# State product ahead of the attention product in a fused attention and expert layer: TensorE's order in a step turned round, the state sum in another bank, and two VectorE operations moved up

## What is computed

```python
q, k = elu(rope(q) * SCALE) + 1, elu(rope(k) * SCALE) + 1          # of layernorm(x) @ w_qkv
kv[t] = kv[t-1] + k[t] (x) v[t];   ks[t] = ks[t-1] + k[t]          # the running state, per head
out[t] = (q[t] @ kv[t]) / max(q[t] . ks[t], 1e-6)
x = x + out @ w_out
h = silu(n @ Wg[e]) * (n @ Wu[e])                                  # n = layernorm(x), e = 0..7
x = x + sum over e of weight[t, e] * (h @ Wd[e])                   # weights from a small router
```

## Time and profile before

| | us |
|---|---|
| median of 3 runs | 805.64 |
| the profiled execution | 806.51 |
| its span, first to last instruction | 804.7 |
| TensorE matmuls (PE) busy | 761.0 (95%) |
| TensorE weight loads (PEld) busy | 655.0 (81%) |
| VectorE (DVE) busy | 603.9 (75%) |
| GpSimd (POOL) busy | 482.7 (60%) |
| ScalarE (ACT) busy | 465.1 (58%) |

### The profile page before, as it was taken

The page is one execution under the profiler, slowest core; times in us unless marked ns, Lnnn a source line. Parts: engine busy times, 40 slices in busy tenths (PEclk is TensorE's granted clock), DMA queues, the critical chain, the costliest instruction groups (busy, mean ns, idle before and its releaser), DMA issues.

```text
span 804.7 us, 18060 instructions
## 1 busy us (share of the span) xinstructions
PE 761.0 (95%) x6660; PEld 655.0 (81%) x6660; DVE 603.9 (75%) x1597; ACT 465.1 (58%) x886; POOL 482.7 (60%) x537
## 2 busy tenths in 40 slices
PE   4475899999999999999999999999999999999998
PEld 3364688888888888888888888888888888888887
DVE  6788797878877797778877697877877788756244
ACT  3664666666666555566665566666656665634222
POOL 3685678765666666556667565565675656653322
PEclk9666799999999999999999999999999999999999
DMA  4644134122210222122111221120211121100000
GB/s 140 128 100 109 43 82 92 41 43 68 40 19 23 44 66 41 41 43 38 44 27 40 43 67 40 41 42 9 60 42 40 40 54 28 28 1 27 1 1 27
DMA packets 97320, 38.27 MB, mean 48 GB/s; under 512 B 74193, under 2 KB 96977, under 8 KB 97233
## 3 DMA queue, kind: packets, MB, share of 16 engines
q1 hardware_dynamic: 90704, 30.83, 17.8%
q10 hardware_dynamic: 6528, 6.29, 2.7%
HBM read 16.13 MB, written 4.19 MB: 25 GB/s over the span
## 4 chain that ended last, share of the span: by engine, by line
PE 88%; DVE 5%; POOL 2%; ACT 2%; issue 1%; DMA 1%; SPq 0%; DVEq 0%; ACTq 0%; POOLq 0%
PE gate L422 22%; PE y L455 22%; PE up L422 21%; PE front L297 5%; PE back L342 3%; PE front L298 3%; PE back L378 2%; PE back L353 2%; PE up L390 1%; PE front L320 1%; PE front L403 1%; PE back L335 1%; PE back L365 1%; POOL a_lo L1167 1%; PE back L320 1%
## 5 line engine op out<-in xcount | busy, mean ns | idle before, releaser
L1196 POOL TENSOR_TENSOR h_lo<-work,h_hi 128x512 fp32r<-128x512 f32 x126 | 163.3, 1296 | 59.7 <-ACT h_hi L657 59.7
L1167 POOL TENSOR_TENSOR a_lo<-am,a_hi 128x512 f16<-128x512 f32 x120 | 144.2, 1203 | 55.3 <-ACT a_hi L584 52.6
L455 PE MATMUL y<-wd_hi,h_hi 128*128 128x256 f32 x504 | 145.8, 289 | 0.0
L455 PE MATMUL y<-wd_lo,h_hi 128*128 128x256 f32 x504 | 141.9, 282 | 0.0
L455 PE MATMUL y<-wd_hi,h_lo 128*128 128x256 f32 x504 | 141.3, 280 | 0.0
L1040 DVE TENSOR_TENSOR work<-work,up 128x512 f32<-128x512 f32 x128 | 87.1, 680 | 70.6 <-PE up L422 70.2
L1056 DVE SCALAR_TENSOR_TENSOR xa<-y,wo,xa 128x256 f32<-128x256 f32 x252 | 111.9, 470 | 2.0 <-PE y L455 2.0
L657 ACT ACTIVATE h_hi<-work 128x512 fp32r<-128x512 f32 x126 | 79.3, 629 | 58.6 <-DVE work L1040 37.0
L455 PEld LDWEIGHTS y<-wd_lo,h_hi 128*128 128x128 f32 x504 | 94.9, 188 | 3.0
L455 PEld LDWEIGHTS y<-wd_hi,h_hi 128*128 128x128 f32 x504 | 95.0, 188 | 2.9
L584 ACT ACTIVATE a_hi<-am 128x512 f16<-128x512 f32 x120 | 74.9, 625 | 35.1 <-DVE am L819 35.0
(11 more groups left out here) (217 smaller groups left out, 1740.2 us busy)
## 6 DMA issues: line engine op xcount, KB each, us to landing
xr<-xT SPq DMA_DIRECT2D x32, 128.0 KB, 2.4
xa<-x SPq DMA_DIRECT2D x32, 128.0 KB, 2.6
out<-xa SPq DMA_DIRECT2D x32, 128.0 KB, 1.7
xa<-Wg ACTq DMA_DIRECT2D x8, 256.0 KB, 3.0
work<-Wd ACTq DMA_DIRECT2D x8, 256.0 KB, 2.7
work<-Wu ACTq DMA_DIRECT2D x8, 256.0 KB, 2.9
work<-w_qkv SPq DMA_DIRECT2D x2, 384.0 KB, 3.8
qT<-q_st SPq DMA_TRANSPOSE x32, 3.2
```

What stands on the lines that cost most here:

```text
L455: m = pe.matmul(y_bank(n, t), h_at(hi, n)[:, t * P:(t + 1) * P], wd_p[wi][:, u // KI, u % KI, :], start=(n % KI == 0 and (t % 2 == 0 or n ...
L1167: pool.tensor_tensor(a_p[1][:, heads(r), :], am_place(g, r).rearrange("p (h n) -> p h n", h=4), a_p[0][:, heads(r), :], ALU.subtract).then ...
L1196: pool.tensor_tensor(h_at(1, n), hb[:, n % 2, :], h_at(0, n).bitcast(F32), ALU.subtract).then_inc(s_hlo, 1)
```

## The change

On TensorE `state(c)` goes from behind `o_T(c)` to the front of `av(c)`. Its sum goes to bank U instead of R2 for tiles from 4 on; so it waits for `h_up(n)`, the last reader of that bank, and `up(n + 1)`, the next writer, waits for `st_add(c)`. Within `av` of those tiles the part from the state comes last instead of first; both halves of the sum are announced by the last two matmuls. On VectorE `h_up(n)` moves from behind `cos(a)` to ahead of `var_eps(a + 1)`, and `st_add(c)` from behind `h_up(n + 1)` to between `cos(a)` and `rope(a)`. The head keeps its order. No instruction is added or taken out but waits.

```diff
+        def state_bank(g):
+            return R2 if g < NT else U
@@ av(g)
-                w.wait_ge(s_s3, g)
                 w.wait_ge(s_amask, 4 * g + 4)
                 w.wait_ge(s_v3, g + 1)
-                for p in range(NP):
-                    for odd in range(2):
-                        rows = slice(64 * odd, 64 * odd + 64)
-                        pe.matmul(BK[odd][:, p * WV:(p + 1) * WV], qT[rows, g % 2, p, :],
-                                  st_x[rows, p, :, :].rearrange("p a b -> p (a b)"),
-                                  start=(p == 0), stop=False, skip_group_check=True)
+                def from_state(first, last):
+                    w.wait_ge(s_s3, g)
+                    for p in range(NP):
+                        for odd in range(2):
+                            rows = slice(64 * odd, 64 * odd + 64)
+                            m = pe.matmul(BK[odd][:, p * WV:(p + 1) * WV], qT[rows, g % 2, p, :],
+                                          st_x[rows, p, :, :].rearrange("p a b -> p (a b)"),
+                                          start=(first and p == 0), stop=(last and p == NP - 1), skip_group_check=True)
+                            if last and p == NP - 1:
+                                m.then_inc(s_av, 1)
+                if g < NT:
+                    from_state(True, False)
                 w.wait_ge(s_alo, 4 * g + 4)
                 for odd in range(2):
                     for p in range(NP):
-                        for a in a_p:
+                        for i, a in enumerate(a_p):
                             m = pe.matmul(BK[odd][:, p * WV:(p + 1) * WV], a[:, 2 * p + odd, :],
                                           vx[:, g % 2, 2 * p + odd, :, :].rearrange("p a b -> p (a b)"),
-                                          start=False, stop=(p == NP - 1), skip_group_check=True)
-                    m.then_inc(s_av, 1)
+                                          start=(g >= NT and p == 0 and i == 0), stop=(g < NT and p == NP - 1),
+                                          skip_group_check=True)
+                    if g < NT:
+                        m.then_inc(s_av, 1)
+                if g >= NT:
+                    from_state(False, True)
@@ state(g)
-                w.wait_ge(s_o, 2 * g + 1)
+                w.wait_ge(s_v3, g + 1)
+                if g < NT:
+                    w.wait_ge(s_o, 2 * g + 1)
+                else:
+                    w.wait_ge(s_h, NT * (g - NT) + 1)
...
-                        m = pe.matmul(R2[:, p * 2 * W1:(p + 1) * 2 * W1],
+                        m = pe.matmul(state_bank(g)[:, p * 2 * W1:(p + 1) * 2 * W1],
@@ up(n)
                 w.wait_ge(s_h, n)
+                w.wait_ge(s_ss, 2 * min((n + NT - 1) // NT + NT, NTL))
@@ TensorE's step
-                logit_rows(router); gate(n); logit(router); up(n); qkv(a); gate(n + 1); av(c); down(n - 2)
-                up(n + 1); down(n - 1); o_T(c); state(c); gate(n + 2); proj(c); up(n + 2); gate(n + 3); down(n)
+                logit_rows(router); gate(n); logit(router); up(n); qkv(a); gate(n + 1); state(c); av(c); down(n - 2)
+                up(n + 1); down(n - 1); o_T(c); gate(n + 2); proj(c); up(n + 2); gate(n + 3); down(n)
@@ VectorE's step
-                mean_var(a + 1); tcos_scale(a); x_lo(a + 1); acc(n - 4, 1); acc(n - 4, 2); acc(n - 4, 3)
-                var_eps(a + 1); route_zone(router); route_nearest(router); cos(a); h_up(n); rope(a); o_sum(c, 0)
+                mean_var(a + 1); tcos_scale(a); x_lo(a + 1); acc(n - 4, 1); acc(n - 4, 2); acc(n - 4, 3); h_up(n)
+                var_eps(a + 1); route_zone(router); route_nearest(router); cos(a); st_add(c); rope(a); o_sum(c, 0)
                 o_sum(c, 1); den_max(c); phi(a); route_weight(router); den_rec(c); slab_lo(slab(s, 1))
                 route_first(router); norm(c); route_second(router); q_lo(a); k_lo(a); o_lo(c); h_up(n + 1)
-                st_add(c); route_tie(router); x1_add(c); acc(n - 2, 0); bn2(c); route_ix2(router); acc(n - 2, 1)
+                route_tie(router); x1_add(c); acc(n - 2, 0); bn2(c); route_ix2(router); acc(n - 2, 1)
```

More of the change, by code:

```diff
@@ L151, in build @@
         oT = R3[:, 0:D].rearrange("p (k n) -> p k n", k=KD)
-        stp = R2[:, 0:NP * 2 * W1].rearrange("p (q h d) -> p q h d", q=NP, h=2)
         io = bcast(iota[:, :], 1, NT)
@@ L847, in st_add @@
                 w.wait_ge(s_state, g + 1)
+                stp = state_bank(g)[:, 0:NP * 2 * W1].rearrange("p (q h d) -> p q h d", q=NP, h=2)
                 for hh in range(2):
```

## The result

The changed kernel takes 804.22 us (median of 14 runs, 803.15 to 805.23) against 805.5 us (14 runs, 804.5 to 807.11); ratio 0.9981, 95% interval 0.9974 to 0.9988. Two more comparisons gave 0.9984 (0.9976 to 0.9993) and 0.9981 (0.9973 to 0.9989). The forecast was 1.8 us less.

The account below looks back on a forecast made before the run. TensorE's matmul sequence was taken as the bound: -2.2 us in steps plus 0.4 early gives -1.8, so 804.7 from the profiled 806.51, and 803.8 us as median, 0.87 lower. Range 801.0 to 806.9 us.

Parts of the forecast that it names:

- The losses between kinds of matmul: TensorE time lost in a steady step when the kind of matmul changes: 0.39 us before, 0.31 us after.
- the rival in which the load goes through while the array empties: Attention product to down costs 0.09 instead of 0.20 us, 3.1 us more gained: 800.7 us; chance 0.12.
- The gain of a steady step: TensorE's fewer losses between kinds of matmul make each step 0.08 us shorter.
- Gate to state product: Loss on TensorE from gate matmuls to the moved state product: taken as 0, farther bound 0.11 us.
- the third rival: `st_add` holds `rope`, so TensorE stands 0.16 to 0.2 us before `proj` in every step: 808.7 us; chance 0.15.
- some 0.2: Time in us until the state product's last matmul is through and signalled to `st_add`, within `rope` being 0.17 late.
- Sum of the early steps: -0.5 + 0.6 + 0.3 = +0.4 us: Steps 5 to 8: step 5 gains 0.5 us, step 6 loses 0.6, steps 7 and 8 lose 0.3.
- the 2.2 us: Forecast gain from 0.08 us less in each of the 28 steps with a tile from 4 on.
- 0.72 less, `norm` some 0.2 later, gain 0.5: Step 5: state product done before TensorE's wait for `norm` costs nothing, `norm` slips some 0.2, gain 0.5 us.
- so about 0.6 stays as a loss: Step 6: state product stands 0.75 us for `h_up`, delaying the chain to the transposed k; about 0.6 us lost.
- Steps 7 and 8: Taken as between step 6 and the steady step; a guessed loss of 0.3 us for both.
- The rival in which the switches only move: Gate to state product costs 0.11 or `o_T` to gate 0.09 us after all: 806.3 to 806.9 us; chance 0.20.

Follow-up runs that it names:

- the sum behind rope: Changed kernel with `st_add` moved behind `rope` on VectorE: 804.85 us, ratio 0.9992; with the attention product also in its old order: 803.95 us, ratio 0.9984.
- the kernel only turned: Kernel before with only the attention product turned round, part from the state last, state product in its old place: 806.42 us, ratio 1.0011.
- early as before: Changed kernel with steps 5 to 8 in the old order, bank and waits: 804.56 us, ratio 0.9986.
- not turned: Changed kernel, state product first, but the attention product in its old order: 803.31 us, ratio 0.9975; again 803.72 us, 0.9971.
- two more changes of rows: Changed kernel with the attention product cut in two by heads, alternating scores' part and part from the state: 810.56 us, ratio 1.0063.
- `h_up` late: Changed kernel with `h_up(n)` back behind `cos(a)`, ahead of `st_add`, on VectorE: 833.18 us, ratio 1.0344.

## Why the prediction was right, and where not

**The losses between kinds of matmul: right.** Every term is within 0.025 us. The rule read from the earlier trace rows, that emptying the array and loading 128-row fp32 weights add up, gave 0.20 and 0.192 was measured; it is what refutes the rival in which the load goes through while the array empties (800.7 us). The Trainium skill (TensorE: Matmul & The Clock Gate, Part 3) allows a load beside running matmuls only for another row group. Across a change of rows the load rows above go with it as far as they reach: the load at 437.90 starts 0.11 behind the last matmul's start, as if held. That the array is empty by then they do not show, since the profile's end of that matmul, a modelled one, is 437.97. Within 128 rows disagree with it, as the prediction says.

**The gain of a steady step: 0.07 to 0.08 us without step 18, 0.05 to 0.06 with it.** Gate to state product was taken as 0 from the transposes' row, and it is 0.022, still nearer the lower of its bounds. With that, 393 - 321 is 0.072 us, or 1.6 us in the 22 steps from 9 to 31, and 1.0 to 1.4 were measured. Another 0.012 a step are lost within `proj` (see the sum behind rope), and 0.35 at `proj` in step 18 of the changed kernel (columns as in the other timelines):

```profile
397.29 0.39 ACT L625 ACTIVATE ox_hi<-back 128x256 fp32r<-128x256 f32 x1 [0.20 <-issue]
396.71 0.69 DVE L829 TENSOR_TENSOR q_st<-front,q_st 128x512 f16<-128x512 f32 x1 [1.59 <-ACT k_st L579]
398.38 0.50 PE L396 MATMUL back<-wout_hi,ox_hi 128*128 128x256 f32 x2
```

Here `q_lo` (line 829) starts 0.46 us after ScalarE's copy of k has ended, 0.10 in the other steps, and the gates ahead end their slots at 398.13: `proj` starts 0.25 late, and its second matmul another 0.10. The step takes 23.01 us, where the quiet steps around it take 22.65. The kernel before had such a delay in step 30 and lost nothing by it. This is the third rival, in one step of the 22. In the third profile step 20 lost 0.3 more, 0.20 of it a wait for the transposed k. Without these steps the others are 0.07 to 0.08 us shorter each than in the kernel before, in all three profiles. The margin was thinner than worked out: `rope` was 0.28 us late, not 0.17 (2.05 behind the last gate pair's start instead of 1.77), and `o_lo` ends 0.15 us ahead of `proj` in nearly every step, where the earlier trace rows have 0.50. VectorE's rows show what `rope` waits for:

```profile
434.91 0.67 DVE L1060 TENSOR_TENSOR work<-work,up 128x512 f32<-128x512 f32 x1
436.98 0.62 DVE L870 SCALAR_TENSOR_TENSOR st_s<-up,st_s 64x136 f32<-64x136 f32 x2 [0.55 <-PE up L371]
437.64 0.69 DVE L813 SCALAR_TENSOR_TENSOR rop<-front,rop 128x512 f32<-128x512 f32 x1
443.25 0.41 DVE L900 TENSOR_TENSOR ox_lo<-back,ox_hi 128x256 fp32r<-128x256 f32 x1
```

`st_add` idles 0.55 for the state product and `rope` follows it at once. The state product's last slot ends at 436.69 and `st_add` starts at 436.98: 0.3 us, where the prediction's sum has "some 0.2". That is the 0.1 by which `rope` is later than told. `h_up` ends at 435.58, well before the state product at 436.06, as predicted.

**The early steps: wrong sign, and both of their large terms wrong.** "Sum of the early steps: -0.5 + 0.6 + 0.3 = +0.4 us"; with the 4 x 0.08 that these steps have in the 2.2 us it is +0.1 for steps 5 to 8, and measured is -0.5 to -0.7. TensorE's waits in steps 5 and 6 of the changed kernel:

```profile
95.77 0.44 PE L383 MATMUL back<-ident,nat 128*128 128x128 f32 x2 [1.65 <-DVE nat L892]
95.96 0.70 PE L440 MATMUL gate<-x_hi,wg_hi 128*128 128x512 f32 x2
98.28 0.50 PE L396 MATMUL back<-wout_hi,ox_hi 128*128 128x256 f32 x2 [0.68 <-DVE ox_lo L900]
114.18 0.76 PE L371 MATMUL up<-vx,k_st 128*128 128x34 bf16 x24 [0.69 <-DVE work L1060]
```

*Step 5, "0.72 less, `norm` some 0.2 later, gain 0.5".* It is 0.75 us shorter in this profile, but not by that sum. In the kernel before the granted clock falls to the lower of its two levels, 1.2 GHz, at 97.1 us, behind the 1.96 us of idle time, and stays there for 3.4 us. The state product and the gates of the earlier trace rows ran at that level, the gates 0.43 us apart. The kernel only turned has the state product in the same old place and waits 1.94 us for `norm`, but its granted clock is 1.00 from 90 to 100 us. `proj` in the kernel before, then `o_T`, gates and `proj` in the kernel only turned:

```profile
100.54 0.41 PE L378 MATMUL back<-wout_hi,ox_hi 128*128 128x256 f32 x2
```

```profile
94.99 0.44 PE L376 MATMUL back<-ident,nat 128*128 128x128 f32 x2 [1.94 <-DVE nat L883]
95.88 0.71 PE L433 MATMUL gate<-x_hi,wg_hi 128*128 128x512 f32 x2
97.53 0.50 PE L389 MATMUL back<-wout_hi,ox_hi 128*128 128x256 f32 x2
```

Counted from the step's first `qkv` matmul (88.54 and 86.69), `proj` starts at 12.01 us in the one and at 10.84 in the other: the lower clock cost 1.17 there. In the changed kernel it starts at 11.13. So at full clock the new order is 0.29 us late at `proj`, not early. The state product is gone from behind `o_T`, but TensorE then waits 0.68 us for `o_lo`, which ends at 11.07 instead of 10.79, because `norm` is 0.31 late. The prediction took its 0.72 us from rows at the lower clock, and it left out this wait. That the kernel only turned still needs 23.31 us for the step comes from a wait of 0.91 us for the transposed k, whose transfer took 5.64 us in its profile and 3.33 in that of before.

Whether the new order keeps the clock up, or chance does, isn't settled. With the old order in step 5 the clock fell there in two profiles (before, early as before) of three, with the new one in none of nine. The timed runs lean the same way: of 70 runs of the kernel before, timed beside the later kernels, 19 have a mean granted clock of 0.967 or 0.968, as those two profiles have (0.968), and of 37 of the changed kernel none. In the two comparisons that had the changed kernel beside them, these runs of before have medians of 805.96 and 806.39 us, the others 805.01 and 805.50, the changed kernel 804.19 and 804.00. That they are the runs with a fall in step 5 is inferred from the mean over the whole program. If they are, some tenths of a us of the measured 1.5 come by the clock.

*Step 6, "so about 0.6 stays as a loss".* The wait for `h_up` is there, 0.69 us, and the chain behind it is late as told: the transposed k is sent off 12.39 us after the step's first `qkv` matmul, 11.42 in the kernel before. But it lands 17.03 us after it, against 16.98. The chain of waits of before and the timeline of after, at that place:

```profile
123.38 5.55 DMA kT<-k_st
```

```profile
126.70 0.28 PE L474 MATMUL y<-wd_hi,h_lo 128*128 128x256 f32 x1
126.91 0.40 PE L323 MATMUL front<-qT,kT 64*128 64x128 f16 x8
```

In the changed kernel the scores follow down at once, without the 0.67 us of the earlier trace rows, and the step takes 23.52 us against 23.44: 0.1 lost instead of 0.6. I had pushed back a transfer of fixed length, 5.55 us, and it took 4.64. The later start isn't what made it shorter: in the third profile of the changed kernel it is sent off at 11.56 and takes 4.60. In this step it took 5.54 to 5.61 in the three kernels with the old order there (before, only turned, early as before), 4.58 to 4.70 in the changed kernel, not turned, with two more changes of rows and with `h_up` late, and 3.66 and 3.57 in the two with the sum behind `rope`, sent off at 11.58 and 11.45. A load of weights (`Wd`) is sent off 0.71 to 0.74 us behind it in the first two groups alike, 1.07 and 1.17 in the last, so that neighbour can't tell the first from the second. The cause stays open. In step 5 the same transfer took 3.3 to 6.35 us, and there it differs between executions of one kernel too; in steps 7 to 9 it took 3.1 to 3.2 in all twelve profiles.

The third profile of the changed kernel divides the two steps otherwise. Step 5 takes 23.70 us, with a wait of 0.99 for the transposed k, and step 6 then has no wait for `h_up` and takes 22.69. Together they are 46.39 us, against 46.19 and 46.16 in the other two and 46.86 before. Steps 7 and 8 lost nothing, where I had guessed 0.3.

**The total** came out by errors of opposite sign, and so by luck: for the steps from 9 on 24 x 0.08 = 1.9 us were forecast and 1.1 to 1.4 came, and steps 5 to 8 gained 0.5 to 0.7 where a loss of 0.1 was forecast, the gain in part by the clock. The rival in which the switches only move is refuted by the table: `o_T` to gate costs 2 ns, gate to the state product 22.

## What to carry to other kernels

On a full TensorE the list of kinds of matmul in order is a budget by itself: each change between 64 and 128 rows and each return from 16-bit to fp32 weights has a price to be read off starts, and putting groups side by side that share type and rows takes one return away without a single instruction less. Such gains are hundredths of a microsecond a step, so compare profiles between the same instructions of the same steps, and not by spans, when the stretch before the change varies by more than the gain. The length of a transfer is no constant of its place: here the same one took 3.6, 4.6 or 5.6 us depending on the kernel, so neither it nor a wait behind it can be carried over as it is. And rows at a lowered clock are no price list: look at the granted clock of the window before a time is taken from it, and compare with a profile in which it did not fall.

## What was not expected of the hardware

- The first 16-bit matmuls on 128 rows come 0.022 us late behind fp32 gate matmuls of 512 columns, and only 0.004 behind fp32 transposes.
- With nearly the same idle time before `o_T` in step 5, 1.96, 1.96 and 1.94 us, the granted clock fell to the lower of its two levels (1.2 GHz, gates 0.43 us apart) in the profiles of before and of early steps as before, and not in that of the kernel only turned. So with this idle time it falls in some executions and not in others.
- The delay in front of `q_lo`, 0.35 us beyond the usual 0.10, lies in the same step, 18, in all ten profiles of kernels with the state product moved from step 9 on, and in step 30 in the two with it in its old place. So it goes with the program and not with the execution. What it is, stays open; no run was made for it.
